# A four-direction selective scan on one core: preparation of the next tile in smaller pieces at other states, the directions' sum added bank by bank, the input term's buffer refilled half by half

## The reference

```python
# x_dbl: projections of the tokens; four directions k (by rows, by columns, and both reversed)
x_dbl = einsum('bkdl,kcd->bkcl', xs, x_proj_w)         # dts (8), Bs (16), Cs (16) per token
delta = softplus(dt_w @ dts + dt_bias)
def step(h, inp):                                      # over 65,536 tokens, for 256 channels x 16 states
    h = exp(delta * A) * h + (delta * x) * B
    y = sum over states of h * C
y = sum over the four directions of y (brought back to one order) + D * x
```

## Time and profile before

| what | value |
|---|---|
| median of three runs | 25194.18 us (25191.23 to 25199.92) |
| profiled execution, span | 25195.8 us, from its first to its last instruction |
| PE, DVE, ACT, POOL busy | 93%, 95%, 92%, 85% of the span |
| the scans | from 3427.7 to 24507.9 us of the span |
| DVE scans L1310 | 19310.1 us busy, 459.5 us idle before them, 440.5 of it until PE's db L1212 |
| PE turn L1209 | 672.5 us idle before, 630.7 of it until DVE's s_h L1310 |
| PE total L1225 | 373.4 us idle before, 356.1 of it until ACT's s_yt L1128 |
| ACT decay L1280 | 564.0 us idle before, 391.9 of it until DVE's s_h L1310 |

### The profile page before, as it was taken

The page is one execution under the profiler, slowest core; times in us unless marked ns, Lnnn a source line. Parts: engine busy times, 40 slices in busy tenths (PEclk is TensorE's granted clock), DMA queues, the critical chain, the costliest instruction groups (busy, mean ns, idle before and its releaser), DMA issues. The chain is left out here.

```text
span 25195.8 us, 507382 instructions
## 1 busy us (share of the span) xinstructions
PE 23521.1 (93%) x189644; PEld 20143.4 (80%) x189644; DVE 23949.9 (95%) x23996; ACT 23136.4 (92%) x46999; POOL 21402.9 (85%) x9612
## 2 busy tenths in 40 slices
PE   4997989999999999999999999999999999999999
PEld 1775468888888888888888888888888888888887
DVE  6998889999999999999999999999999999999996
ACT  3997579999999999999999999999999999999986
POOL 5000059999999999999999999999999999999997
PEclk8998999999999999999999999999999999999999
DMA  5212654444444455555555555555555555555555
GB/s 179 61 58 97 188 175 169 168 168 169 167 169 169 166 180 180 181 179 180 181 180 179 178 181 183 180 180 182 181 181 176 183 181 180 183 180 181 182 181 189
DMA packets 2918626, 4287.64 MB, mean 170 GB/s; under 512 B 1199806, under 2 KB 2251106, under 8 KB 2636258
## 3 DMA queue, kind: packets, MB, share of 16 engines
q1 hardware_dynamic: 2916194, 4255.17, 50.8%
HBM read 3660.03 MB, written 594.54 MB: 169 GB/s over the span
## 5 line engine op out<-in xcount | busy, mean ns | idle before, releaser
L1310 DVE TENSOR_TENSOR_SCAN s_h<-s_da,s_h,s_db 128x512 f32<-128x512 f32 x16256 | 19310.1, 1257 | 459.5 <-PE s_db L1212 440.5
L1327 POOL TENSOR_TENSOR s_prod<-s_h,s_cb 128x2048 f32<-128x2048 f32 x4096 | 18716.0, 4569 | 101.7 <-issue 47.5
L1280 ACT ACTIVATE s_da<-s_delta,a_neg 128x512 f32<-128x512 f32 x16384 | 10907.1, 716 | 564.0 <-DVE s_h L1310 391.9
L1269 ACT ACTIVATE s_dxb<-s_dx,s_btok 128x256 f32<-128x256 f32 x20480 | 9019.3, 501 | 27.7 <-PEq L59 27.7
L1225 PE MATMUL s_py<-eye,s_prod 128*128 128x128 f32 x65536 | 8511.0, 273 | 373.4 <-ACT s_yt L1128 356.1
L1209 PE MATMUL s_db<-eye,s_dxb 128*128 128x128 f32 x49152 | 8188.6, 276 | 672.5 <-DVE s_h L1310 630.7
L1225 PEld LDWEIGHTS s_py<-eye,s_prod 128*128 128x128 f32 x65536 | 7414.0, 141 | 457.9 <-issue 438.0
L1209 PEld LDWEIGHTS s_db<-eye,s_dxb 128*128 128x128 f32 x49152 | 5740.8, 142 | 2192.9 <-issue 1524.1
L1212 PE MATMUL s_db<-s_bdiag,s_dx 128*128 128x128 f32 x32768 | 6338.3, 275 | 0.0
L1212 PEld LDWEIGHTS s_db<-s_bdiag,s_dx 128*128 128x128 f32 x32768 | 4951.4, 191 | 0.0
L1340 POOL TENSOR_SCALAR s_dxb<-s_dx,s_btok 128x256 f32<-128x256 f32 x4096 | 1994.7, 487 | 531.7 <-PE s_db L1212 454.8
(11 more groups left out here) (135 smaller groups left out, 16294.0 us busy)
## 6 DMA issues: line engine op xcount, KB each, us to landing
s_cb<-c_rows SPq DMA_DIRECT2D x2048, 1024.0 KB, 4.8
s_bdiag<-b_diag SPq DMA_DIRECT2D x2048, 256.0 KB, 4.8
s_xt<-xc_tok SPq DMA_DIRECT2D x1024, 256.0 KB, 5.3
y<-s_yt SPq DMA_DIRECT2D x1024, 256.0 KB, 2.6
s_xc<-xc_own SPq DMA_DIRECT2D x384, 512.0 KB, 6.5
s_yb<-y SPq DMA_DIRECT2D x768, 256.0 KB, 3.9
xc_tok<-c_ot SPq DMA_DIRECT2D x32, 2048.0 KB, 8.5
xc_own<-s_xc SPq DMA_DIRECT2D x128, 512.0 KB, 5.9
```

Source lines behind the costliest of these rows:

```text
L1269: last = e.activation(dxb[:, i % NDXB, j, :], dx[:, g % 2, j, :], ACT.Copy, scale=btok[:, g % 2, j, n:n + 1])
L1280: last = e.activation(da[:, i % NDA, half, :], delta[:, g % 2, half, :], ACT.Exp, scale=wts[k]["a_neg"][:, half, n:n + 1])
L1310: last = e.tensor_tensor_scan(h[:, n, half, flow], da[:, i % NDA, half, flow], db[:, i % NDB, half, flow], first, ALU.mult, ALU.add)
L1327: e.tensor_tensor(prod[:, p % GROUPS_KEPT], h[:, states], cb[:, states, :].unsqueeze(2).to_broadcast([P, TOGETHER, HALVES, T]), ALU.mult). ...
```

## The change

Four things are done:

1. The number of the state at which a stage is called is replaced by tables (`PLAN_KEPT` for tiles whose xc is loaded, `PLAN_TURNED` for those of direction 1, and one of each for the first tile to be prepared in a direction). A negative number means that many states before the end of the tile before. The projection is cut in two pieces of 256 tokens: at states 14 (of the tile before) and 0 instead of both at 2; in direction 1 at 1 and 3, with the transposes at state 14 and their copy at 15 of the tile before. low is at 2 instead of 3 (direction 1: 4). In direction 1 the later stages are one state later. low also waits for the store of the B rows of the tile before.
2. The sum of the directions is added bank by bank (`ADDED`): after totals 5 and 9 in direction 1, after totals 8 and 14 in directions 2 and 3, instead of both after total 8.
3. The scan increments its semaphore after each half, and `turn` waits for each half by itself, in front of that half's transposes, instead of for both in front of the first.
4. At n = 4 ACT's `leave` comes before scale(i+2) and decay(i+2) instead of after them.

```diff
+    ADDED = {1: (5, 9), 2: (8, 14), 3: (8, 14)}
...
-            elif stage == 2:
...
+            elif stage in ("proj0", "proj1"):
+                part = slice(0, T // 2) if stage == "proj0" else slice(T // 2, T)
+                if stage == "proj0":
+                    if kept:
+                        e.wait_ge(S[f"xld{s}"], kept * DMA)
+                        if n > 1:
+                            e.wait_ge(S["dx"], n - 1)
+                    else:
+                        e.wait_ge(S["xc"], turns)
                 for half in range(HALVES):
-                    last = e.matmul(pr[0:ROWS_ALL, 0, :], w["proj"][:, half, :], xc[:, s, half, :],
+                    last = e.matmul(pr[0:ROWS_ALL, 0, part], w["proj"][:, half, :], xc[:, s, half, part],
                                     start=(half == 0), stop=(half == HALVES - 1))
-                last.then_inc(S["proj"], 1)
+                if stage == "proj1":
+                    last.then_inc(S["proj"], 1)
...
+        PLAN_KEPT = {
+            "PE": {-2: "proj0", 0: "proj1", 4: "turnb", 6: "dts", 10: "turnd"},
+            "ACT": {2: "low", 7: "exp", 8: "log"},
+            "DVE": {5: "btok", 9: "delta", 11: "dx"},
+        }
+        PLAN_KEPT_FIRST = {
+            "PE": {1: "proj0", 2: "proj1", 4: "turnb", 6: "dts", 10: "turnd"},
+            "ACT": {3: "low", 7: "exp", 8: "log"},
+            "DVE": {5: "btok", 9: "delta", 11: "dx"},
+        }
+        PLAN_TURNED = {
+            "PE": {-2: "turned", 1: "proj0", 3: "proj1", 5: "turnb", 7: "dts", 11: "turnd"},
+            "ACT": {-1: "xc", 4: "low", 8: "exp", 9: "log"},
+            "DVE": {6: "btok", 10: "delta", 12: "dx"},
+        }
...
+            def due(engine, g, n):
+
+                for tile, at in ((g + 1, n), (g + 2, n - D_STATE)):
+                    if prepares(tile) and at in plan(tile)[engine]:
+                        yield tile, plan(tile)[engine][at]
+
+            def scanned(e, i, half):
+
+                e.wait_ge(S["h"], HALVES * i + half + 1)
...
-                        if i >= NDB:
-                            e.wait_ge(S["h"], i - NDB + 1)
                         for half in range(HALVES):
+                            if i >= NDB:
+                                scanned(e, i - NDB, half)
                             for j in range(SUBS_ACT):
                                 e.transpose(db[:, i % NDB, half, j * P:(j + 1) * P],
...
-                        if k and n == 2 * GROUP:
-                            e.wait_ge(S[f"before{g % 2}"], LINES * DMA * (g // 2 + 1))
-                            for bank in range(2):
+                        for bank in range(2):
+                            if k and n == ADDED[k][bank]:
+                                if bank == 0:
+                                    e.wait_ge(S[f"before{g % 2}"], LINES * DMA * (g // 2 + 1))
                                 subs = slice(bank * SUBS // 2, (bank + 1) * SUBS // 2)
...
-                        if prepares(g + 1):
-                            prepare_pe(e, weights(g + 1), kept(g + 1), turns(g + 1), g + 1, g + 1, n)
+                        for tile, stage in due("PE", g, n):
+                            prepare_pe(e, weights(tile), kept(tile), turns(tile), tile, tile, stage)
...
                         g, n = divmod(i, D_STATE)
+                        if g >= 1 and n == LAG:
+                            for bank in range(2):
+                                leave(e, g - 1, bank)
                         if i + AHEAD < STEPS:
                             scale(i + AHEAD)
                             decay(i + AHEAD)
...
-                        if g >= 1 and n == LAG:
-                            for bank in range(2):
-                                leave(e, g - 1, bank)
...
-                            if half == HALVES - 1:
-                                last.then_inc(S["h"], 1)
+                            last.then_inc(S["h"], 1)
```

More of the change, by code:

```diff
@@ L947, in prepare_pe @@
             s = g % 2
-            if stage == 0 and not kept:
+            if stage == "turned":
                 e.wait_ge(S[f"load{s}"], LINES * DMA * ((n + 1) // 2))
@@ L955, in prepare_pe @@
                 last.then_inc(S["turned"], 1)
-            elif stage == 2:
[L957 to L962, removed]
+            elif stage in ("proj0", "proj1"):
[7 more added lines that the diff above has]
+                        e.wait_ge(S["xc"], turns)
                 for half in range(HALVES):
-                    last = e.matmul(pr[0:ROWS_ALL, 0, :], w["proj"][:, half, :], xc[:, s, half, :],
+                    last = e.matmul(pr[0:ROWS_ALL, 0, part], w["proj"][:, half, :], xc[:, s, half, part],
                                     start=(half == 0), stop=(half == HALVES - 1))
-                last.then_inc(S["proj"], 1)
-            elif stage == 4:
+                if stage == "proj1":
+                    last.then_inc(S["proj"], 1)
+            elif stage == "turnb":
                 e.wait_ge(S["low"], n)
@@ L972, in prepare_pe @@
                 last.then_inc(S["turnb"], 1)
-            elif stage == 6:
+            elif stage == "dts":
                 e.wait_ge(S["btok"], n)
@@ L978, in prepare_pe @@
                              start=True, stop=True).then_inc(S["dts"], 1)
-            elif stage == 10:
+            elif stage == "turnd":
                 e.wait_ge(S["delta"], n)
@@ L988, in prepare_act @@
             s = g % 2
-            if stage == 1 and not kept:
+            if stage == "xc":
                 e.wait_ge(S["turned"], turns)
@@ L993, in prepare_act @@
                 e.copy(xc[:, s], pr[:, :, :]).then_inc(S["xc"], 1)
-            elif stage == 3:
+            elif stage == "low":
                 e.wait_ge(S["proj"], n)
@@ L1012, in prepare_dve @@
             s = g % 2
-            if stage == 5:
+            if stage == "btok":
                 e.wait_ge(S["turnb"], n)
@@ L1019, in prepare_dve @@
                 e.tensor_copy(btok[:, s], rows[:, :, B_ROW:B_ROW + D_STATE]).then_inc(S["btok"], 1)
-            elif stage == 9:
+            elif stage == "delta":
                 e.wait_ge(S["log"], n)
@@ L1030, in prepare_dve @@
                 e.tensor_tensor(flat(dx[:, s]), flat(pr[:, :, :]), flat(xt[:, s]), ALU.mult).then_inc(S["dx"], 1)
-        STAGES = 12
+        PLAN_KEPT = {
[13 more added lines that the diff above has]
+        }
+        PLAN_TURNED_FIRST = {
+            "PE": {0: "turned", 2: "proj0", 3: "proj1", 5: "turnb", 7: "dts", 11: "turnd"},
+            "ACT": {1: "xc", 4: "low", 8: "exp", 9: "log"},
+            "DVE": {6: "btok", 10: "delta", 12: "dx"},
+        }
         with nc.Block() as block:
@@ L1060, in _ @@
             def _(e):
-                for stage in range(STAGES):
+                for stage in PLAN_KEPT_FIRST["PE"].values():
                     prepare_pe(e, wts[0], 1, 0, 0, 1, stage)
@@ L1065, in _ @@
             def _(e):
-                for stage in range(STAGES):
+                for stage in PLAN_KEPT_FIRST["ACT"].values():
                     prepare_act(e, wts[0], 1, 0, 0, 1, stage)
@@ L1070, in _ @@
             def _(e):
-                for stage in range(STAGES):
+                for stage in PLAN_KEPT_FIRST["DVE"].values():
                     prepare_dve(e, 0, 1, stage)
@@ L1235, in total @@
                                                 start=False, stop=False, skip_group_check=True)
-                            last.then_inc(S["added"], 1)
+                                if bank == 1:
+                                    last.then_inc(S["added"], 1)
                         if n == GROUP and k in SKIP:
@@ L1277, in decay @@
                         if i >= NDA:
-                            e.wait_ge(S["h"], i - NDA + 1)
+                            scanned(e, i - NDA, HALVES - 1)
                         for half in range(HALVES):
@@ L1291, in _ @@
                             decay(i + AHEAD)
-                        if prepares(g + 1):
-                            prepare_act(e, weights(g + 1), kept(g + 1), turns(g + 1), g + 1, g + 1, n)
-                        if g >= 1 and n == LAG:
-                            for bank in range(2):
-                                leave(e, g - 1, bank)
+                        for tile, stage in due("ACT", g, n):
+                            prepare_act(e, weights(tile), kept(tile), turns(tile), tile, tile, stage)
                     for bank in range(2):
@@ L1311, in _ @@
                                                         first, ALU.mult, ALU.add)
-                            if half == HALVES - 1:
-                                last.then_inc(S["h"], 1)
-                        if prepares(g + 1):
-                            prepare_dve(e, g + 1, g + 1, n)
+                            last.then_inc(S["h"], 1)
+                        for tile, stage in due("DVE", g, n):
+                            prepare_dve(e, tile, tile, stage)
                 @block.gpsimd
@@ L1323, in product @@
```

(2 more changed lines are left out.)

11 lines of the change are left out of this document (8 added, 3 removed).

## The result

The changed kernel takes 24590.34 us (median of 4 runs, 24587.79 to 24592.47) against 25193.98 (25191.23 to 25199.92): a ratio of 0.976, 95% interval 0.9748 to 0.9772. It is 604 us faster; 505 were forecast, and the low end of the range was 24,630.

A forecast was written before the change was run, and what follows sets the result against it. DVE, 95% busy, was taken as the bound, with POOL's floor equal; closing DVE's waits for PE saves 1.02 + 1.12 + 2 x 0.92 = 3.98 us, times 127 tiles 505 us: 25,194 to 24,689, range 24,630 to 24,870.

The forecast's parts named there:

- the low end of the range: Whole kernel: all tiles at 40.03 save 544 us, to 24,650, less some 20 for first tiles: 24,630.
- all three gaps: DVE's idle before states 4, 6 and 8 (0.12, 0.45, 0.45 us a tile, together 1.02), all forecast to close.
- The sum, 3.98 us over four tiles: Savings per tile: direction 0 1.02, direction 1 1.12, directions 2 and 3 0.92 each; times 127 tiles, 505 us.
- DVE's floor is 41.05 - 1.02 = 40.03.: DVE's tile of 41.05 us less 1.02 of idle places: a floor of 40.03 us a tile.
- 0.10 a tile: Directions 2 and 3: copy starts 0.07 us late, delaying delta; with 0.03 more allowed, 0.10 a tile.
- the middle of 40.03 and 40.23: Direction 1's tile, between DVE's floor and ACT's busy time, which includes the copy of xc: 40.13 us.
- The prediction's first bound: DVE's waits, window less busy time: at most 125 to 151 us per direction can be won.
- Weight loads: Split projection on PE: doubled loads taken as 0 extra; the skill's rule would cost 0.56 us a tile.
- Rival 1: Directions 2 and 3 pay for PE's pieces ahead of the copy: tile 40.66, total 24,823; chance 0.13.
- rival 2: POOL becomes the bound, one wait of 0.33 left making every tile 40.35: 24,813; chance 0.10.
- Rival 3: Gap before state 6 or 8 stays since ACT gives scale(6) later: half the gain, 24,942; chance 0.06.
- Rival 4: The wait inside each turn costs PE, slower from 0.09 us a turn: 26,510; chance 0.03.

The follow-up runs named there:

- H: The half-by-half refill (turn waits for each scan half by itself) alone, added to the kernel before: 25012.16 us, ratio 0.9932.
- C: ACT's copy of the sums put ahead of scale and decay, alone, added to the kernel before: 25162.11 us, ratio 0.9988.
- P: The plans (new states of the preparation, projection in two) alone, added to the kernel before: 24853.9 us, ratio 0.9868.
- P and C together: The kernel before with the new plans and the copy first; sum and refill as before: 24596.66 us, ratio 0.9764.
- S: The sum of directions bank by bank; not run alone. The changed kernel without the half-by-half refill, which includes it: 24733.48 us, ratio 0.982.

## Why the prediction was right or wrong

**The mechanism was right, the size of the floor was wrong.** DVE's waits for db were what could be won; all three gaps closed; PE's wait for the copy turned into the copy's wait for PE, in directions 2 and 3 only; the last total started at 8.53 against 8.58. The sum, 3.98 us over four tiles, should have been 41.05 - 39.88 for direction 0, 41.25 - 39.90 for direction 1, and 41.05 - 39.91 for each of the others: 1.17 + 1.35 + 1.14 + 1.14 = 4.80, times 127 610. Two terms were mis-sized:

- *"DVE's floor is 41.05 - 1.02 = 40.03."* It is 39.88. The gap before state 6 was counted from btok's end; the next scan does not wait for that end but starts 0.12 after btok's start, so the gap was 0.53 (0.54 in most tiles), not 0.45. Another 0.05 are the first steps behind two of the gaps (1.20 instead of 1.17), which went with them, and 0.01 is rounding (41.04). The range's low end was built on 40.03 in every tile, and this is why the measured time lies below it.
- *"0.10 a tile"* for directions 2 and 3, and *"the middle of 40.03 and 40.23"* for direction 1. The allowances were not needed. With both halves of the sum added after total 8, so that neither stands right before the copy, the time is the same; and ACT's busy time, tails included, overstated ACT, which just keeps up in direction 1.

Per set of four tiles that is 0.15 x 4 + 0.10 x 3 = 0.90, less 0.08 because directions 1 to 3 end 0.02 or 0.03 above 39.88: 0.82, times 127 104 us. The medians are 99 apart from the forecast, the profiled spans 102.

The prediction's first bound failed by the same cause. It said that at most 125 to 151 us per direction could be won from DVE's waits, the window less DVE's busy time; 144 to 171 were won. DVE's busy time itself fell with the waits, from 5142.46 to 5103.86 us in direction 0 for the same work, 0.30 a tile. In a row of scans a record's last 0.08 us lies under the next one's start and counts once; before a gap it counts as busy, three times a tile, and the two slow first steps add 0.05.

**Weight loads.** The Trainium skill's rule ("TensorE: Matmul & The Clock Gate", The mechanism) that loads overlap matmuls only in other row groups would have made the split projection 0.56 dearer. In the changed kernel a projection piece starts at 19029.86 and the next turn at 19030.72: 0.86, half of 1.72, with the loads under the running matmuls:

```profile
19029.86 0.58 PEld L967 LDWEIGHTS s_pr<-s_xc,w_proj 128*73 128x73 f32 x3
```

The rows do not agree with the rule. Rival 1 is out: tiles of directions 2 and 3 are 39.91, not 40.66.

**The rivals.** POOL (rival 2) was a fair fear: it is a bound, but at the same height as DVE, and its wait of 0.33 vanished with PE's lateness. Rival 3 is out (no gap stays); with the copy first alone a late ACT did take the gain back, but through the logarithm, not through scale(6). Rival 4 is out (its 1.4 us under the tile is 1.6 for direction 1's 41.25, which changes little): a turn costs PE 1.10 as before when its waits are met, and about 0.06 more a half when not (three transposes in 0.55 instead of 0.49).

**What was not foreseen: what each part is worth.** The prediction added up gaps for the whole and gave no part a price of its own. The runs give these, each against the kernel before: H -179, C -29, P -337; P and C together -594; all four -604. Adding S to P and C costs 137 (24596.66 to 24733.48), and H pays it back (to 24590.34). So the states of the projection and the place of ACT's copy are the change. In directions 2 and 3 the sum by banks puts 0.86 us of PE's work before the copy, and the refill hides it again. By itself the sum brought nothing in any direction (direction 1 has 40.04 with and without it when the refill is left out), and the refill's own gain on top of P and C is direction 1's 40.04 to 39.90, about 18 us.

Why P and C together are worth 228 us more than their sum shows in DVE's rows. P alone closes the gaps before states 4 and 6 and leaves the one before 8, since PE then stands for the copy. C alone takes that stand away, but its copy waits for a last total that the projection still makes late, and DVE waits before delta instead. Each part removes what the other leaves.

## What to carry to other kernels

Before giving a late engine more buffer, find which of its instructions stands at the wrong place. Here 1.72 us of work that could be done earlier was moved away from just before a hand-over, and the hand-over was put first in the other engine's queue; together this gave 594 of 604 us, while a finer refill of the buffer alone gave 179. Parts of such a change do not add up (337 and 29 alone, 594 together), so undo each from the whole as well as trying each alone, and look where the wait went when a part seems to bring nothing. Count a floor from start to start, not from durations or busy time: here a scan's record ends 0.08 us after the next one has started.

## What the runs showed of the hardware

- A nearly full TensorE can lose its clock in single tiles: with the refill and without the copy first, PE's wait in direction 0 grew from 0.97 to 1.57 us, its granted clock fell to 0.98 on the mean (0.89 in a window of 10 us), and the 50 tiles with a drop took 41.87 us instead of 40.35, 76 us in all. The wait alone does not decide it: 76 tiles with the same wait, and all of direction 1 with 1.62 us, kept 1.00. PE was busy for 0.93 of direction 0 and 0.96 of direction 1; whether that is the reason is not shown.
- The scans' mean recorded duration rose from 1257 to 1314 ns while their steps stayed at 1.17 us and the tiles became shorter. The long records lie in direction 0 of the changed kernel's trace (1470 ns on the mean, 1258 to 1264 in the other three); there those of DVE and ACT end up to half a us later (btok at 8465.33 is 0.67 long, and the next scan starts at 8465.44 all the same). Such records also hide short idle times, so two traces are compared by their steps, not by mean durations or busy shares.
- DVE and POOL each stood at 39.9 us a tile; relieving one gave 10 or 13 us, relieving both 347, none of it in direction 1, where ACT stood at 39.90 as well.
